# Layers 1 and 2 of a gather-scatter kernel: block places kept in fixed registers across the loop's turn

## The reference

```
s2, d2 = concat([src, dst]), concat([dst, src])
for l in range(3):
    e_in = concat([h_prev[s2], h_prev[d2], ef2])
    msg = leaky_relu(e_in @ We1[l]) @ We2[l]
    red = segment_sum(msg, d2, N)
    out = leaky_relu(concat([h_prev, red]) @ Wn1[l]) @ Wn2[l]
    h_prev = out + h_prev
return layernorm(x + out)
```

## Time and profile before

| what | value |
|---|---|
| median of 3 runs | 3841.99 us (3841.14 to 3844.13) |
| the profiled execution's own time | 3845.63 us |
| its span, first to last instruction | 3843.8 us |
| TensorE matmuls busy | 2487.5 us, 65% |
| VectorE busy | 2776.0 us, 72% |
| ScalarE busy | 2124.5 us, 55% |
| edge loop of layer 0 | about 1316 to 2152 us |
| layer 1, from its tables on | about 2205 to 2972 us |
| layer 2, from its tables on | about 3019 to 3788 us |

### The profile page before, as it was taken

One profiled execution on the slowest core, in us unless ns is written; L12 is line 12 of the kernel. 1 busy time (PEld: TensorE's weight loads), 2 busy tenths in 40 slices (PEclk: granted clock), 3 DMA queues, 4 the chain that ended last, 5 costly groups with the idle time before them and its releaser, 6 DMA issues.

```text
span 3843.8 us, 81410 instructions
## 1 busy us (share of the span) xinstructions
PE 2487.5 (65%) x27206; PEld 2149.4 (56%) x27207; DVE 2776.0 (72%) x3367; ACT 2124.5 (55%) x4171; POOL 776.4 (20%) x826
## 2 busy tenths in 40 slices
PE   4000000000015589999999699999999799999996
PEld 4000000000015577777777488888888588888884
DVE  8965565566423699999999677777777677777775
ACT  4000000000003577777777578888888688888884
POOL 0577777777751000000000000000000000000000
PEclk9555555555557799999999899999999899999998
DMA  8111111111026467777677345555554255555553
GB/s 240 55 41 32 43 43 31 43 43 31 16 45 158 116 232 242 244 240 239 240 243 240 132 165 181 181 181 182 188 180 168 88 182 190 180 180 186 183 182 109
DMA packets 202979, 566.31 MB, mean 147 GB/s; under 512 B 38553, under 2 KB 79839, under 8 KB 200895
## 3 DMA queue, kind: packets, MB, share of 16 engines
q1 hardware_dynamic: 175390, 550.42, 43.0%
q0 software_dynamic: 27552, 15.37, 2.1%
HBM read 407.88 MB, written 157.93 MB: 147 GB/s over the span
## 4 chain that ended last, share of the span: by engine, by line
PE 45%; DMA 11%; DVE 6%; issue 5%; SPq 2%; ACT 1%; POOL 0%; DVEq 0%; ACTq 0%; POOLq 0%
PE gath L1305 16%; PE sums L1367 11%; DMA fchunk<-feat_d 8%; PE sums L1305 8%; PE gath L1298 4%; PE sums L1298 2%; DMA recc<-records 2%; DVE big L1031 2%; PE sums L1240 1%; DVE loop_buf L1101 1%; DVE gsel L1035 1%; ACT big L755 1%; SPq L542 1%; PE sums L1465 1%; PE sums L1260 1%
## 5 line engine op out<-in xcount | busy, mean ns | idle before, releaser
L1031 DVE SCALAR_TENSOR_TENSOR big<-big 128x768 f32<-128x768 f32 (+1 forms) x957 | 909.5, 951 | 479.4 <-ACT big L755 437.8
L1305 PE MATMUL gath<-table,gsel 128*128 x7488 | 1079.0, 273 | 0.0
L1101 DVE TENSOR_TENSOR loop_buf<-big,loop_buf 128x768 f16<-128x768 f32 x936 | 891.2, 952 | 0.0
L630 POOL DMA_INDIRECT records<-rec,rowi x784 | 750.7, 958 | 284.6 <-issue 247.3
L1367 PE MATMUL sums<-loop_buf 128*128 128x128 f16 x11232 | 782.3, 219 | 29.0 <-issue 25.8
L1305 PEld LDWEIGHTS gath<-table,gsel 128*128 128x128 f16 x7488 | 734.6, 98 | 85.0
L759 ACT ACTIVATE loop_buf<-big 128x768 f16<-128x768 f32 x936 | 782.0, 835 | 0.0
L1367 PEld LDWEIGHTS sums<-loop_buf 128*128 128x128 f16 x11232 | 649.1, 98 | 125.3 <-ACT sums L753 36.9
L755 ACT ACTIVATE big<-gath 128x512 f32<-128x512 f32 x936 | 559.6, 598 | 283.8 <-PE gath L1305 283.8
L1221 PE MATMUL sums<-table,fchunk 128*128 128x200 f16 x196 | 37.1, 365 | 877.1 <-DVE found L944 864.6
L1305 PE MATMUL sums<-table,gsel 128*128 x3744 | 564.5, 274 | 0.8 <-DMA gsel<-gsel_d 0.4
(11 more groups left out here) (175 smaller groups left out, 1868.5 us busy)
## 6 DMA issues: line engine op xcount, KB each, us to landing
gsel<-gsel_d SPq DMA_DIRECT2D x208, 576.0 KB, 3.8
loop_buf<-ssel_d SPq DMA_DIRECT2D x208, 576.0 KB, 5.3
numb<-nums_d SPq DMA_DIRECT2D x106, 576.0 KB, 4.7
gsel_d<-gsel SPq DMA_DIRECT2D x104, 576.0 KB, 5.6
ssel_d<-loop_buf SPq DMA_DIRECT2D x104, 576.0 KB, 6.5
fchunk<-feat_d SPq DMA_DIRECT2D x313, 144.0 KB, 3.0
loop_buf<-rows_d SPq DMA_DIRECT2D x28, 896.0 KB, 4.8
records<-rec,rowi POOLq DMA_INDIRECT x784
```

What stands on the lines that cost most here:

```text
L630: pool.indirect_dma_start(out=records[:, :], out_offset=bass.IndirectOffsetOnAxis(ap=rowi[:, h, g:g + 1].bitcast(U32), axis=0), in_=rec[:, ...
L1031: return dve.scalar_tensor_tensor(m, m, SLOPE, m, ALU.mult, ALU.max)
L1101: dve.tensor_tensor(m_lo[:, place, :], msg[:, place, :], m_hi[:, place, :], ALU.subtract)\
L1305: return pe.matmul(uv, gsel[:, h, (2 * tc + s) * P:(2 * tc + s + 1) * P], at[n], start=False, stop=n == 3, skip_group_check=True)
```

## The change

Three lists of 12 registers, `kept[0]`, `kept[1]`, `kept[2]`, are allocated once, outside the loops. Row j of a pass belongs to `kept[-j % 12]`, so rows 10, 11 and 12 go to `kept[2]`, `kept[1]` and `kept[0]`, where the next pass reads them as its rows -2, -1 and 0. Before the loop these three rows are loaded once in each layer. In the body, rows 1 to 9 are loaded into fresh registers as before, in the odd steps 1 to 17; rows 10, 11 and 12 into the kept ones in steps 19, 21 and 23. `before_last` is gone, and nothing is loaded at the body's head or between the tiles of steps 0 and 1. An `Else` branch, for a pass whose second turn is not live, loads the three rows. In `step`, the call of `before_sums` now stands behind the making of the six sum addresses, in layer 0 as well. `map_row` is 12 words a row longer.

```diff
-        map_row = sb("map_row", [LOADS, (1 + MAP_TURNS) * LOAD_WORDS], I32)
+        map_row = sb("map_row", [LOADS, (2 + MAP_TURNS) * LOAD_WORDS], I32)
...
+            kept = [[pe.alloc_register(f"place_{j}_{k}") for k in range(LOAD_WORDS)] for j in range(1 + LAG_LOADS)]
...
-                    before_last(q)
                     rows2 = gather_rows(places, t + 2)
...
-                    before_sums(q)
                     for i in range(STEP):
                         at = places(t + i - STEP * LAG)
                         for s in (1, 0):
                             sum_at[i, s] = lowered(place_of(at[s]))
+                    before_sums(q)
                     place = (q - LAG) % RING
                     pe.wait_ge(gath6_free, free6)
...
+                    def row_words(j, turn_n):
+
+                        return map_row[j % LOADS:j % LOADS + 1, ds((turn_n + 1 + j // LOADS) * LOAD_WORDS, LOAD_WORDS)]
+
...
+                    def keep_row(j, turn_n):
+
+                        pe.reg_load(kept[-j % (2 * LOADS)], row_words(j, turn_n))
+
+                    for j in range(-LAG_LOADS, 1):
+                        keep_row(j, 0)
                     with nc.Fori(0, -(-TURNS // 2), engines=(mybir.EngineType.PE,), hint_back_edge=True) as it:
                         with pe.If(it * 2 < live_n):
                             step0 = pe.snap(l * live_n * STEPS + it * (2 * STEPS))
                             turn = pe.snap((l * live_n + it * 2) * PER_TURN)
-                            node = {}
-
-                            def load_places(j):
...
-                            def next_places(q):
-
-                                if q % LOAD_STEPS == LOAD_STEPS - 1 and q < 2 * STEPS - 1:
-                                    load_places((q + 1) // LOAD_STEPS)
-
-                            def lag_places(q):
-
-                                if q < LAG_LOADS:
-                                    load_places(q - LAG_LOADS)
-
-                            load_places(0)
+                            loaded = {}
+
+                            def next_row(q):
+
+                                j = (q + 1) // LOAD_STEPS
+                                if q % LOAD_STEPS == LOAD_STEPS - 1 and j < 2 * LOADS - LAG_LOADS:
+                                    _, loaded[j] = nc.values_load_multi_w_load_instructions(
+                                        row_words(j, it * 2), engines=(mybir.EngineType.PE,),
...
+                                elif q % LOAD_STEPS == LOAD_STEPS - 1:
+                                    keep_row(j, it * 2)
+
...
                             for q in range(STEPS):
-                                step(q, loaded, step0, turn, next_places, lag_places)
+                                step(q, places_at, step0, turn, next_row)
                             with pe.If(it * 2 + 1 < live_n):
                                 for q in range(STEPS, 2 * STEPS):
-                                    step(q, loaded, step0, turn, next_places)
+                                    step(q, places_at, step0, turn, next_row)
+                            with pe.Else():
+                                for j in range(-LAG_LOADS, 1):
+                                    keep_row(j, 0)
```

More of the change, by code:

```diff
@@ L1310, in gather_rows, with step @@
                     return [lowered(row(place, s, half)) for s, place in enumerate(places(t)) for half in range(2)]
-                def step(q, places, step0, turn, before_sums, before_last=lambda q: None):
+                def step(q, places, step0, turn, before_sums):
                     p = q // PART_STEPS
@@ L1421, in _, with bounded @@
                 with pe.If(l > 0):
+                    def row_words(j, turn_n):
+                        return map_row[j % LOADS:j % LOADS + 1, ds((turn_n + 1 + j // LOADS) * LOAD_WORDS, LOAD_WORDS)]
+                    def bounded(place):
+                        return place.with_bounds(min_val=0, max_val=(NB - 1) * NODE_BYTES, guaranteed_mod_val=0,
+                                                 out_of_modulus=NODE_BYTES)
+                    def keep_row(j, turn_n):
+                        pe.reg_load(kept[-j % (2 * LOADS)], row_words(j, turn_n))
+                    for j in range(-LAG_LOADS, 1):
+                        keep_row(j, 0)
                     with nc.Fori(0, -(-TURNS // 2), engines=(mybir.EngineType.PE,), hint_back_edge=True) as it:
@@ L1440, in loaded @@
-                            def loaded(t):
-                                return node[t, 0], node[t, 1]
-                            def next_places(q):
-                                if q % LOAD_STEPS == LOAD_STEPS - 1 and q < 2 * STEPS - 1:
-                                    load_places((q + 1) // LOAD_STEPS)
-                            def lag_places(q):
-                                if q < LAG_LOADS:
-                                    load_places(q - LAG_LOADS)
-                            load_places(0)
+                            loaded = {}
@@ new lines, in next_row @@
+                            def next_row(q):
[3 more added lines that the diff above has]
+                                        row_words(j, it * 2), engines=(mybir.EngineType.PE,),
+                                        min_val=0, max_val=(NB - 1) * NODE_BYTES,
+                                        skip_runtime_bounds_check_because="sums of the constant steps over the first buckets")
+                                elif q % LOAD_STEPS == LOAD_STEPS - 1:
+                                    keep_row(j, it * 2)
@@ L1455, in _, with places_at @@
+                            def places_at(t):
+                                j, k = divmod(2 * t, LOAD_WORDS)
+                                row_at = loaded.get(j) or [bass.RuntimeValue.of_register_unchecked(r)
+                                                           for r in kept[-j % (2 * LOADS)]]
+                                return [bounded(place) for place in row_at[k:k + 2]]
                             for q in range(STEPS):
-                                step(q, loaded, step0, turn, next_places, lag_places)
+                                step(q, places_at, step0, turn, next_row)
```

## The result

The changed kernel takes **3792.11 us**, median of 4 runs (3789.6 to 3795.21), against 3841.56 of before (4 runs); the ratio is 0.9873, 95% interval 0.986 to 0.9887. The forecast was 3796.1 with 3786 to 3811.

A forecast was written before the change was run, and what follows sets the result against it. PE was taken to set the pace, only its idle time winnable. Gains of 2.07 us a turn, 49.7 over 24 turns, less 4.2 at entries, plus 0.4, made 45.9: median 3841.99 to 3796.1 us, range 3786 to 3811.

The forecast's parts named there:

- Where the time was: Loop of layers 1 and 2: PE loses 2.70 us a pass at the turn and steps 0 and 1, nothing elsewhere.
- Row 0's load: At the turn: moving this load with its address to step 23 gains 1.05 us a turn (0.62 to 1.18).
- Rival 1: At the turn: a load is cheap (0.62) and the rest of the turn dear, time 3804.7; chance 0.11.
- Rows -2 and -1: Steps 0 and 1: without these loads the stalls of 0.23 and 0.89 go, gaining 1.12 us a turn.
- Step 23's cover: Ahead of step 23's sums: waits hide the moved load, cost 0, or 0.2 if the cover is short.
- Rival 2: Ahead of step 23's sums: the moved load shows by up to 0.3 a turn, time 3803; chance 0.09.
- The entries: Ahead of the loop in layers 1 and 2: two loads more cost 2.1 us a layer, 4.2 in all.
- The first passes: Steps 0 and 1 of each layer's first pass: little gained, only 0.39 us in layer 2.
- the two fetches: High end of the range: one code fetch more in each layer's entry, 6.6 us together.
- Rival 4: Loop body no longer stays in the sequencer's memory: each turn pays a 3.3 us code fetch, 3875, slower; chance 0.03.
- Rival 5: Copies between registers at each turn or use eat the gain, time within 0.2% of before; chance 0.03.

The follow-up runs named there:

- row0_head: The changed kernel with the control's raised counts, row 0 loaded at the head of the loop body again and not in step 23: 3821.91 us, ratio to before 0.9947.
- the control: The changed kernel with the two counts read at run time raised to at least 1 by a register operation: 3793.04 us.
- jump_only: The kernel before with only an Else branch that never runs added behind its second half turn, one jump more a turn: 3847.35 us, ratio to before 1.0018.

## Why the prediction was right

- **Where the time was** (the turn and steps 0 and 1, 2.70 a pass, nothing elsewhere): right in the main. Steps 0 and 1 are clean, the turn is nearly the only loss left. The exceptions are the few late steps 9 and 15; in one of them, in the kernel before, PE did idle 0.23 for a DMA, where the prediction says never.
- **Row 0's load**, 1.05 by two intervals: 1.04 by one edit, 1.00 by three loads in a row. The reasoning that a sequencer stops at a wait, and that what is behind a wait in series is paid in full, held. Rival 1 (0.62) is out.
- **Rows -2 and -1**, 1.12 a turn: 1.12 in the changed kernel, 1.18 a pass when put back. Right.
- **Step 23's cover**: it held in all 26 passes. What it has to spare was not measured. Rival 2 is out.
- **The entries**, 4.2 lost, because each load ahead of the loop was to cost 1.05 there as at the turn: this failed. The two entries got 1.5 shorter. The seven kernels with three loads ahead of the loop and none at the head have 4.7 to 5.2 in layer 1 and 7.6 to 8.5 in layer 2. The three with one at the head and none ahead, before and the two made from it, have 5.7 to 6.0 and 8.8 to 9.2. With one at the head and two ahead (`row0_head`) it is 5.97 and 8.68, so two loads more ahead of the loop cost nothing beyond that scatter. A load at the head costs up to 1.0 in an entry too: 5.97 for the control's 4.96, and three of them 2.99 and 2.46. Hidden loads ahead of the loop were the lower bound only in the prediction. That they hide behind the fetching of code is argued: one instruction packet comes in layer 1's entry and two in layer 2's, in both kernels, but no run moved them.
- **The first passes**, 0.4 won: it was 1.5.
- **Rival 4** (code fetched in each turn): no instruction packet in the loop. **Rival 5**: the page counts 72 instructions fewer than before (81338 for 81410), where copies of 36 registers a pass would have added hundreds.

The misses went opposite ways: 3.6 lost at the turns, 5.7 won at the entries and 1.1 in the first passes. Their sum turns the forecast gain of 45.9 into 49.1, and the medians differ by 49.5. So the mechanism at the turn was right, but that the time is only 4 us off is in part luck: two terms were wrong, and they partly cancelled. The high end of the range, 3811, holds rival 1 and the two fetches alone; with rival 2 on top, as its text has it, it would be about 3818.

## What to carry to other kernels

"Issue" idle time on the bounding engine is sequencer work, and its price can be had from the trace: find two intervals with the same register work, one released by a wait whose end is known. Then move what is dear (register loads) ahead of a wait that the engine stands at anyway, and keep what nothing covers, a loop's turn above all, free of loads and of taken jumps. An `Else` that never runs is paid for by the path that does.

## What the runs showed of the hardware

- A register load of 12 aligned words costs the sequencer 1.00 to 1.04 with its address, 4 words 0.51, 2 words 0.77. Nothing behind it passes it.
- A taken jump over one instruction costs 0.25 at a turn. An If that falls through, its comparison included, costs 0.07.
- Loads ahead of a loop, in the microseconds in which instruction packets come, cost nothing that can be seen; at the head of its body they cost up to 1.0 each.
- After 3.6 us without a matmul the granted clock fell to the lower level in 16 of 24 cases, for about one step, 1.6 us each. After two idle times of 1.3 and 1.4 us with one group of sums between them it did in 4 of 24. After a single one of 1.4 or 1.7 us (`before`, `jump_only`, `row0_head`) it did in none of 72.
